# 144 extra matmuls on a constant tile behind the broadcasts of each layer norm, in an eight-core transformer block

## What is computed

```python
x = x + attn(layernorm(x))          # Wqkv shared by the heads; mask multiplies before softmax
f = layernorm(x)
w = top2_weights(softmax(f @ router_w + router_b))
x = x + gelu(f @ sw1 + sb1) @ sw2 + sb2 \
      + sum_e w[:, e] * (gelu(f @ rw1[e] + rb1[e]) @ rw2[e] + rb2[e])
```

## Time and profile before

| | us |
|---|---|
| two runs of the kernel | 3805.4 and 3885.7 |
| their median | 3845.5 |
| the profiled execution | 3805.6 |
| its span, slowest core (core 4) | 3804.0 |
| spans of the eight cores | 3799.2 to 3804.0 |

### The profile page before, as it was taken

The page is one execution under the profiler, slowest core; times in us unless marked ns, Lnnn a source line. Parts: engine busy times, 40 slices in busy tenths (PEclk is TensorE's granted clock), DMA queues, the critical chain, the costliest instruction groups (busy, mean ns, idle before and its releaser), DMA issues.

```text
span 3804.0 us, 44158 instructions; the slowest of 8 cores (3799.2 to 3804.0 us)
## 1 busy us (share of the span) xinstructions
PE 2870.4 (75%) x15189; PEld 1359.9 (36%) x15380; DVE 1164.9 (31%) x2358; ACT 840.2 (22%) x1354; POOL 28.8 (1%) x55
## 2 busy tenths in 40 slices
PE   2354555555544545847999999999999999999997
PEld 0222222222222223313444444444444444444443
DVE  5222222222222222261233333333233333323332
ACT  0233233222332332002112122111212212121210
POOL 0000000000000000000000000000000000000000
PEclk7555555555555555868999999999999999999998
DMA  2100000000000000050050220403122050222202
GB/s 90 29 1 1 1 1 1 1 1 1 1 1 1 1 1 1 1 89 1 1 84 7 45 45 13 77 1 61 29 45 45 1 89 1 45 45 42 48 1 89
DMA packets 7081, 98.18 MB, mean 26 GB/s; under 512 B 1860, under 2 KB 2260, under 8 KB 2388
## 3 DMA queue, kind: packets, MB, share of 16 engines
q0 software_dynamic: 3984, 77.81, 12.6%
q1 hardware_dynamic: 2884, 17.53, 1.4%
HBM read 164.58 MB, written 8.39 MB: 45 GB/s over the span
## 4 chain that ended last, share of the span: by engine, by line
PE 71%; DVE 12%; issue 7%; ACT 6%; DMA 1%; DVEq 1%; SPq 0%; ACTq 0%; POOL 0%
PE PM L747 26%; PE PM L834 26%; PE PS L441 6%; DVE SMASK L421 5%; PE PS L402 4%; ACT PTB L426 2%; ACT PTA L426 2%; DVE AVN L458 2%; PE PTR L465 2%; PE PS L344 2%; ACT PTB L412 2%; PE PS L508 2%; DVE RZ L453 1%; PE PS L370 1%; PE PS L361 1%
## 5 line engine op out<-in xcount | busy, mean ns | idle before, releaser
L747 PE MATMUL PM<-XLN,W 128*128 128x512 bf16 x4515 | 1009.6, 383 | 20.6 <-DVE WB L892 14.4
L834 PE MATMUL PM<-H1G,W 128*128 128x512 bf16 x4516 | 994.1, 379 | 4.8
L764 ACT ACTIVATE H1G<-PM,B1C 128x512 bf16<-128x512 f32 x576 | 395.8, 687 | 1573.4 <-PE PM L747 1573.4
L747 PEld LDWEIGHTS PM<-XLN,W 128*128 128x128 bf16 x4608 | 454.0, 99 | 573.0 <-issue 54.4
L834 PEld LDWEIGHTS PM<-H1G,W 128*128 128x128 bf16 x4608 | 450.9, 98 | 543.7
L813 DVE TENSOR_TENSOR H1G<-H1G,WB 128x512 bf16<-128x512 bf16 x512 | 217.8, 425 | 675.5 <-ACT H1G L764 675.5
L849 DVE TENSOR_TENSOR XRES<-XRES,PM 128x512 f32<-128x512 f32 x288 | 198.2, 688 | 652.3 <-PE PM L834 652.3
L465 PE MATMUL PTR<-IDB,AVN 128*64 128x128 bf16 x256 | 68.5, 268 | 321.3 <-DVE AVN L458 321.3
L421 DVE TENSOR_TENSOR SMASK<-PS,MASKS 128x512 f32<-128x512 f32 x256 | 177.0, 691 | 375.9 <-ACT PTB L412 137.0
L402 PE MATMUL PS<-QT,KT 64*128 64x512 bf16 x640 | 284.4, 628 | 0.0
L441 PE MATMUL PS<-VA,PTB 128*128 128x65 bf16 x1536 | 97.4, 242 | 190.6 <-ACT PTB L426 190.6
(11 more groups left out here) (103 smaller groups left out, 1120.0 us busy)
## 6 DMA issues: line engine op xcount, KB each, us to landing
W<-w1cat POOLq DMA_DIRECT2D x9, 4096.0 KB, 28.6
W<-w2cat POOLq DMA_DIRECT2D x9, 4096.0 KB, 28.9
XRES<-xt SPq DMA_DIRECT2D x8, 1024.0 KB
ot<-XRES SPq DMA_DIRECT2D x8, 1024.0 KB
WRF<-wr_rl POOLq DMA_DIRECT2D x1, 2048.0 KB, 16.8
MASKS<-c_masks SPq DMA_DIRECT2D x1, 512.0 KB
B1C<-b1col POOLq DMA_DIRECT2D x9, 8.0 KB, 28.0
B2C<-b2col_t POOLq DMA_DIRECT2D x9, 4.0 KB, 1.9
```

Source lines behind the costliest of these rows:

```text
L747: lambda e, psv=psv, kc=kc, ht=ht, tt=tt: e.matmul(psv, W1[:, kc * DFF + ht * 128: kc * DFF + (ht + 1) * 128], xln(kc)[:, tt * 512:(tt + 1 ...
L764: lambda e, h1sl=h1sl, psv=psv, e_i=e_i, ht=ht: e.activation(h1sl, psv, AF.Gelu, bias=B1C[:, (e_i % 2) * 16 + ht: (e_i % 2) * 16 + ht + 1]),
L834: lambda e, psv=psv, kc=kc, dtl=dtl, buf=buf: e.matmul(psv, W2[:, kc * D + dtl * 128: kc * D + (dtl + 1) * 128], H1G[:, buf * 8192 + kc * 512:
```

## The change

In emit_ln, between cb2 and the sixteen operations of L248 and L252, TensorE gets 144 more matmuls. Each takes one row of ONES as weights (128 columns) and one row of ONES as moving data (512 columns) and overwrites one of the four pieces of PB1 in turn. The first waits for cb2, by which PB1 has been read; the last increments ST. Nothing reads what they write. As emit_ln is called twice, the program gets 288 of them. The name kw_last is not used further, and no other line changes; but counts of ST taken behind these lines, by barrier() and by the load of IDF, are one higher for each call and so include them.

```diff
                     cb2 = P.emit("vector",
                             lambda e: e.tensor_copy(B2SB[:], PB2[:]),
                             waits=[("SV", cb1)], inc="SV")
+                    kw_last = 0
+                    for kwi in range(144):
+                        kw_last = P.emit("tensor",
+                                lambda e, kwi=kwi: e.matmul(
+                                    PB1[:, (kwi % 4) * 512:(kwi % 4) * 512 + 512],
+                                    ONES[0:1, 0:128], ONES[0:1, 0:512],
+                                    start=True, stop=True),
+                                waits=([("SV", cb2)] if kwi == 0 else []),
+                                inc=("ST" if kwi == 143 else None))
                     applied = []
                     prev = cb2
```

## The result

| | before | changed |
|---|---|---|
| profiled execution, us | 3805.6 | 3871.4 |
| its span, slowest core, us | 3804.0 | 3869.9 |
| lowest run, us | 3805.2 | 3870.9 |
| median of all runs, us | 3881.1 (10 runs) | 3936.2 (11 runs) |

The ratio as computed is 1.019 with a 95% interval of 1.013 to 1.025: slower, by an amount that lies around 2%. It counts five runs of the changed kernel, of which four lie at 3870.9 to 3872.1 us and one at 3910.8. The profiled executions differ by 65.8 us, a ratio of 1.017; the forecast was 66.6. The median of all runs is 3936 us, outside the range of 3860 to 3915. In many executions of either kernel two or more cores show a lower granted clock and run up to 11% longer, and a median over all runs depends on how many of them there are. What follows compares profiled executions.

What follows compares the result with a forecast made beforehand. VectorE was taken to bound both layer norms, covering about 30 us of TensorE work in each, at clock 0.50. Delays of 32.0 + 34.6 = 66.6 us on 3805.6 gave 3872 us (added as 66.4), range 3860 to 3915.

Steps and rivals of the forecast that it cites:

- Price of one, hidden weight loads: Added matmuls in both layer norms: 0.427 us each at the low clock, weight loads hidden behind the matmul before.
- The rival in which loads come on top: Both layer norms: unhidden weight loads add up to 0.15 us each, 43 us, 3915 us at most; 4 in 100.
- Which clock: Under the added matmuls: clock stays at 0.50 throughout, as matmuls that feed few rows do not raise it.
- The case of the risen clock: Rival, both layer norms: clock rises under the added matmuls, cost about 9 us, time 3815 us; 7 in 100.
- First layer norm: Barrier behind ln1: TensorE arrives last, at 135.6 instead of 103.6 us, delaying all loads behind it by 32.0 us.
- Second: Second layer norm: router matmuls queue behind the 144, then run back to back; bias matmul L601 34.6 us later.
- The load of IDF: Router: issued near 1728 instead of 1696.30 us, but covered by about 5 us of work; uncovered it would cost 2 us.
- Downstream: nothing: Attention and expert stage: no gain booked from a raised clock; a warm expert start worth 2.8 us at most.
- The sum: Whole kernel: 32.0 + 34.6 = 66.6 us for the two layer norms, giving 3872 us.
- the last term of the range: Whole kernel's range: a median of few runs may stand 40 us above its profiled execution, giving 3912.
- A clock that lives on into attention: Rival, attention: clock at 1.00 from 122 us on gains some 120 us, about 3695 us; 1 in 100.
- Within 2%: Whole kernel: measured time within 2% either way of before, 0.87; slower by more 0.12, faster by more 0.01.

Runs made afterwards that it cites:

- the run with the clock up to its start: Changed kernel with 128-row matmuls, 120 in the first layer norm, 80 behind its barrier, none in the second: 3804.4 us profiled; a second run 4066.8.
- one of the runs: Changed kernel with the 144 one-row matmuls in the first layer norm only: 3834.9 us.
- the first experiments: Follow-ups on the changed kernel; the one with nine runs of before beside it had 64 added matmuls per layer norm instead of 144: ratio 1.004 to before.
- the 7 beside the last: Runs of the kernel before, measured beside its version with load WRF issued behind the three bias loads on its own semaphore, which took 3792.4 us profiled.

## Why the prediction was right and where it was wrong

- *Price of one, hidden weight loads.* Right: 61.59 us for 144, 0.428 us each with the last one's end, forecast 0.427. The rival in which loads come on top is out.
- *Which clock.* Right, and for the reason given: 0.50 with 1 row and with 64 rows, 1.00 with 128 rows in the same place. The rule of the Trainium skill weighed there, "activity releases the throttle" (page TensorE: Matmul & The Clock Gate, section What's actually happening), agrees with the trace for matmuls of 128 rows and disagrees for those of 1 and of 64. The case of the risen clock was priced at 3815 us from rows, and the run with 128 rows took 3813.
- *First layer norm.* 32.0 forecast, 31.9 measured, as a block shift of all loads. *Second.* 34.6 forecast, 34.5 measured, with the router's eight matmuls back to back (3.50 us). The load of IDF stayed covered: from the bias matmul to the expert stage it is 50.5 us (1763.16 to 1813.67) against 51.0 (1696.77 to 1747.77).
- *Downstream: nothing.* Right: attention 1428.4 us (154.15 to 1582.6) against 1428.8, and the run with the clock up to its start won 1.2 us. VectorE was not slowed either: 28.14 us in both kernels. What the prediction did not have is that the clock falls in attention without an idle gap too.
- *The sum.* 66.6 forecast, 65.8 measured on profiled executions. (The prediction adds 66.4 to 3805.6 where its sum says 66.6; that is 0.2 us and changes nothing.) The two parts are right in the trace to 0.1 us each; that the totals agree within 1 us is also luck, as the expert stage alone came out 4 us shorter in one of the runs.
- *The step that failed* is the last term of the range: "A median of few runs may stand higher above its profiled execution, as it does today by 40 us: that gives 3912." The lift of 40 us came from two runs, 3805 and 3886 us, and was taken as an upper bound. The lift measured is 65 us for the changed kernel (3936.2 against 3871.4). For the kernel before it was 75 us in the 10 runs beside the changed one (median 3881), 11 in the 9 runs beside the first experiments (3816) and 1 in the 7 beside the last (3806), with single runs up to 4201 us. So 40 was one draw from a wide spread and no bound; with 75 instead the upper edge would have been 3947, which is said with hindsight. The mechanism and its size are not touched: five runs of the changed kernel lie at 3870.9 to 3872.1, the profiled one among them, beside 3872 forecast. What lengthens the long runs stays open. That the change itself makes them more frequent is not shown: 6 of 11 runs against 6 of 10 are more than 1.5% above the fastest.
- *The rivals.* A clock that lives on into attention is excluded by the run made for it, weight loads on top by the spacing, and the clock did not rise; none of the three came true.
- *Chances.* "Within 2%" had 0.87. The ratio of 1.019 lies there, but its interval reaches over 2%, and the forecast stood close enough to that bound (1.017) for the chance of slower to deserve more than 0.12.

## What to carry to other kernels

Filler matmuls behind a wait cost only what sticks out beyond the cover: count them at the clock that they themselves will see (64 at 0.427 us were free under 29.8 us, 144 cost 32 to 35). Before paying for a warm-up, look in the profile at which matmuls kept TensorE fully busy at the low clock: here those of 1 and 64 rows did, so they could neither raise it nor hold it. Then ask whether the stage behind would hold the high clock. When a barrier stands in front of loads, look at which of them the first matmul really needs, since that order was worth 13 us and the clock nothing.

## What was unexpected of the hardware

The clock falls while TensorE is fully busy. In the run with the clock up to attention it was 1.00 on core 0 at 126.90 to 129.90 us, with matmuls of 64 rows and of one row back to back (2.96 of 3.00 us busy), and 0.50 from 130 us on under the same matmuls. The prediction had rows for such a fall only beside idle time. The moment differs between the cores of one execution: 1.9 us behind the first QKV matmul on core 6, 6.1 us on core 0.
